# Integer feed-forward of a fused layer stack: gate products first, up products inside the sigmoid pass

## What is computed

```python
def act_qdq(x):
    qmax = 2.0 ** (ACT_BITS - 1) - 1.0
    scale = jnp.maximum(jnp.max(jnp.abs(x)) / qmax, 1e-12)
    return jnp.clip(jnp.round(x / scale), -qmax - 1.0, qmax) * scale
...
x = act_qdq(x)
up = act_qdq(x @ lpbq_dequant(w_up).T)
gate = act_qdq(x @ lpbq_dequant(w_gate).T)
sig = fixed_qdq_u16(jax.nn.sigmoid(gate))
gate = act_qdq(gate * sig)
o = act_qdq(gate * up)
return o @ lpbq_dequant(w_down).T
```

## Time and profile before

| | us |
|---|---|
| median of 3 runs | 2077.92 |
| lowest and highest | 2074.67, 2086.87 |
| span of the profiled execution, first to last instruction | 2076.4 |
| stretch with the gate and up block | 1437 to 1532 |
| stretch with the first gating pass | 1532 to 1573 |
| stretch with the second gating pass | 1573 to 1608 |

### The profile page before, as it was taken

One profiled execution on the slowest core, in us unless ns is written; L12 is line 12 of the kernel. 1 busy time (PEld: TensorE's weight loads), 2 busy tenths in 40 slices (PEclk: granted clock), 3 DMA queues, 4 the chain that ended last, 5 costly groups with the idle time before them and its releaser, 6 DMA issues. The chain is left out here.

```text
span 2076.4 us, 39090 instructions
## 1 busy us (share of the span) xinstructions
PE 1875.1 (90%) x13707; PEld 1519.3 (73%) x13708; DVE 1271.4 (61%) x4668; ACT 835.2 (40%) x2278; POOL 274.0 (13%) x498
## 2 busy tenths in 40 slices
PE   8899998999998989999999988997952989999978
PEld 6567666776767979999999977875531877777745
DVE  7878867778873541111111145676769529999988
ACT  3433336556652111111111102773477524444468
POOL 2001112000001160000000063331000230000022
PEclk9999999999997999999999998998975989999989
DMA  6211111211104421231222021111000031111100
GB/s 224 87 59 47 46 51 67 82 41 42 59 24 155 154 98 59 86 103 66 86 83 86 23 68 42 45 45 62 0 0 0 1 93 44 36 37 39 23 11 31
DMA packets 106722, 124.95 MB, mean 60 GB/s; under 512 B 36160, under 2 KB 85832, under 8 KB 104776
## 3 DMA queue, kind: packets, MB, share of 16 engines
q1 hardware_dynamic: 95704, 107.64, 15.6%
q0 software_dynamic: 3072, 8.39, 1.3%
q10 hardware_dynamic: 7792, 6.95, 1.0%
HBM read 86.39 MB, written 36.63 MB: 59 GB/s over the span
## 5 line engine op out<-in xcount | busy, mean ns | idle before, releaser
L1788 DVE TENSOR_TENSOR me_h<-me_sg,me_ps_u 128x512 f32<-128x512 f32 x106 | 72.5, 686 | 287.3 <-PE me_ps_u L1611 272.0
L1744 ACT ACTIVATE me_sg<-me_ps_g 128x512 f32<-128x512 f32 x106 | 63.3, 597 | 370.4 <-PE me_ps_g L1611 340.3
L1276 ACT ACTIVATE ca_e<-ca_scored,ca_neg_max 128x256 f32<-128x256 f32 x256 | 127.2, 499 | 109.1 <-DVE ca_neg_max L1335 109.1
L1611 PE MATMUL me_ps_g<-me_x_turned,me_w 128*128 128x128 f32 x1184 | 144.8, 276 | 1.9 <-issue 1.9
L1611 PE MATMUL me_ps_u<-me_x_turned,me_w 128*128 128x128 f32 x1184 | 145.4, 276 | 0.0
L1611 PEld LDWEIGHTS me_ps_g<-me_x_turned,me_w 128*128 128x128 f32 x1184 | 141.2, 192 | 4.2 <-issue 2.1
L1618 PE MATMUL me_ps_y<-me_w,me_h 128*128 128x256 f32 x592 | 140.0, 379 | 0.0
L1611 PEld LDWEIGHTS me_ps_u<-me_x_turned,me_w 128*128 128x128 f32 x1184 | 139.4, 193 | 0.0
L2979 ACT ACTIVATE sc_y_all<-ss_v 128x16 f32<-128x16 f32 x256 | 60.8, 238 | 156.1 <-DVE ss_v L3042 156.1
L1618 PEld LDWEIGHTS me_ps_y<-me_w,me_h 128*128 128x128 f32 x592 | 106.8, 190 | 11.4
L1335 DVE CUSTOM_DVE_ANT_0 ca_scored<-ca_main,ca_mask_add 128x256 f32<-128x256 f32 x256 | 92.9, 418 | 20.9 <-PE ca_main L1219 20.9
(11 more groups left out here) (444 smaller groups left out, 4371.6 us busy)
## 6 DMA issues: line engine op xcount, KB each, us to landing
me_w<-in_L_ffn_w_e SPq DMA_DIRECT2D x24, 1024.0 KB, 7.5
ca_k_list<-kv_out SPq DMA_DIRECT2D x28, 256.0 KB, 2.3
ca_v_list<-kv_out SPq DMA_DIRECT2D x28, 256.0 KB, 2.3
sk_gb<-scan_g_band SPq DMA_DIRECT2D x14, 512.0 KB, 3.7
moe_x_list<-me_zeros SPq DMA_DIRECT2D x1, 5248.0 KB, 21.1
me_x_tile<-moe_x_list SPq DMA_DIRECT2D x38, 128.0 KB, 2.0
moe_y_list<-me_y ACTq DMA_DIRECT2D x37, 128.0 KB, 1.7
ca_kT<-ca_k_list SPq DMA_DIRECT2D x4, 1024.0 KB, 4.9
```

Of the source, the lines that this page charges most:

```text
L1276: nc.scalar.activation(e[:, g % 3, e_, it, :], scored[:, g % 2, e_, it, :], ACT.Exp, scale=-1.0, bias=neg_max[:, g % 2, n:n + 1], accum_ou ...
L1611: last = nc.tensor.matmul(ps[:, j * P:(j + 1) * P], w[:, n, kt, f:f + P], x[:, kt, :], start=(kt == 0), stop=(kt == KD - 1))
L1744: nc.scalar.activation(sg[:, c, :], ps_g[c][:, :], ACT.Silu).then_inc(done, 1)
L1788: nc.vector.tensor_tensor(h[:, c, :, :].rearrange("p j n -> p (j n)"), sg[:, c, :], ps_u[c][:, :], ALU.mult).then_inc(done[c], 1)
```

## The change

The two blocks `int_gate_up` and `int_gating` become one, `int_gate_first`, with tile prefix `ig`, no barrier inside it.

- First loop: TensorE makes the gate products alone, one accumulator of 768 columns (two banks) per tile, two such accumulators in turn, filled by pieces of 512 and 256 columns. VectorE takes one maximum over 768 columns per tile and ScalarE makes one copy. x transposed is kept for all tiles, in the place of x normalised.
- The sums and the clipping of the next layer's weights come in this loop. The weights lie in the upper half of `up`, which is not yet used then.
- The scale of gate alone is made. Then the second loop: the sigmoid pass as before, and beside it the up products: TensorE multiplies, VectorE takes the maximum, ScalarE copies. All 16 groups of the next layer's weights are turned in this loop, one per tile.
- The scales of gate * sig and of up are made together, in four VectorE steps on two columns.
- Third loop: the pass with up, as before, but with all up integers made in it. The filler matmuls wait for the product of tile 12 of this loop.

```diff
-        int_gate_up(nc, core, ins, wT, scal, magic, gate, up, tern)
-        int_gating(nc, core, scal, magic, gate, up, tern)
+        int_gate_first(nc, core, ins, wT, scal, magic, gate, up, tern)
         int_down(nc, core, tg, wdT, scal, magic, gate)
...
+def int_gate_first(nc, core, ins, wT, scal, magic, gate, up, tern):
...
+    RING = 4
+    WARM = 28
+    WARM_AT = TILES - 4
+    CUTS = ((0, 512), (512, FF))
...
+        nat = up[:, TILES // 2:TILES, :].rearrange("p t f -> p (t f)").rearrange("p (w n) -> p w n", w=3)
+        xT = core.xn
...
+        ps = [st.ps(f"ps{j}", [P, 1024]) for j in range(2)]
+        next_ps = [st.ps(f"next{j}", [P, 512]) for j in range(2)]
+        idle = st.ps("idle", [P, 512])
...
+            def turn_x(t):
+                pe.wait_ge(x_ready, t + 1)
+                if t >= 1:
+                    pe.wait_ge(xT_ready, t)
+                for kt in range(KD):
+                    last = nc.tensor.transpose(ps_x[:, kt * P:(kt + 1) * P], xi[:, t % 2, kt * P:(kt + 1) * P],
+                                               core.ident[:, :])
+                last.then_inc(x_ps, 1)
+            def multiply(w, t, done):
+                for lo, hi in CUTS:
+                    for kt in range(KD):
+                        last = nc.tensor.matmul(ps[t % 2][:, lo:hi], xT[:, t, kt * P:(kt + 1) * P], wT[:, w, kt, lo:hi],
+                                                start=(kt == 0), stop=(kt == KD - 1))
+                last.then_inc(done, 1)
+            def gate_product(t):
+                pe.wait_ge(xT_ready, t + 1)
+                if t >= 2:
+                    pe.wait_ge(gate_kept, t - 1)
+                multiply(0, t, gate_mm)
+            def up_product(t):
+                if t < 2:
+                    pe.wait_ge(gate_kept, TILES + t - 1)
+                else:
+                    pe.wait_ge(up_kept, t - 1)
+                multiply(1, t, up_mm)
+            def turn_next(g):
+                blocks = parts[g][0]
+                if g >= 2:
+                    pe.wait_ge(copied, g - 1)
+                for j, src in enumerate(blocks):
+                    last = nc.tensor.matmul(next_ps[g % 2][:, j * P:(j + 1) * P], src, ident16[:, :],
+                                            start=True, stop=True)
+                last.then_inc(filled, 1)
+            pe.wait_ge(x_max, 1)
+            nc.tensor.transpose(ps_x[0:1, 0:P], xmax[:, :], core.ident[:, :]).then_inc(x_row, 1)
+            pe.wait_ge(x_one, 1)
+            nc.tensor.matmul(ps[0][:, 0:1], one[:, :], xone[:, :], start=True, stop=True).then_inc(x_all, 1)
+            pe.wait_ge(xsteps, 2)
+            turn_x(0)
+            for t in range(TILES):
+                if t + 1 < TILES:
+                    turn_x(t + 1)
+                gate_product(t)
+            pe.wait_ge(ident_ready, 1)
+            for t in range(TILES):
+                up_product(t)
+                turn_next(t)
+            pe.wait_ge(product, TILES + WARM_AT)
+            for _ in range(WARM):
+                nc.tensor.matmul(idle[:, 0:P], core.ident[:, :], core.ident[:, :], start=True, stop=True)
...
+            def copy_x(t):
+                act.wait_ge(x_ps, t + 1)
+                nc.scalar.activation(xT[:, t, :], ps_x[:, 0:D], ACT.Copy).then_inc(xT_ready, 1)
+            def keep_gate(t):
+                act.wait_ge(gate_maxed, t + 1)
+                nc.scalar.activation(gate[:, t, :], ps[t % 2][:, 0:FF], ACT.Copy).then_inc(gate_kept, 1)
+            def keep_up(t):
+                act.wait_ge(up_maxed, t + 1)
+                nc.scalar.activation(up[:, t, :], ps[t % 2][:, 0:FF], ACT.Copy).then_inc(up_kept, 1)
...
+            def copy_next(g):
+                out = parts[g][1]
+                act.wait_ge(filled, g + 1)
+                nc.scalar.activation(out, next_ps[g % 2][:, 0:out.shape[1]], ACT.Copy).then_inc(copied, 1)
...
+            for u in range(TILES + 1):
+                if u < TILES:
+                    copy_x(u)
+                if u >= 2:
+                    keep_gate(u - 2)
+                if u in (9, 11, 13):
+                    ternary((u - 9) // 2)
+            nc.scalar.preload_act_table(ACT.Sigmoid)
+            keep_gate(TILES - 1)
+            act.wait_ge(gate_scaled, 1)
+            integers(0)
+            for t in range(TILES):
+                if t + 1 < TILES:
+                    integers(t + 1)
+                sigmoid(t)
+                keep_up(t)
+                if t >= 1:
+                    copy_next(t - 1)
+            copy_next(TILES - 1)
+            act.wait_ge(all_scaled, 1)
+            for t in range(TILES):
+                gate_integers(t)
+                up_integers(t)
...
+            def gate_max(t):
+                dve.wait_ge(gate_mm, t + 1)
+                nc.vector.tensor_reduce(gate_top[:, t:t + 1], ps[t % 2][:, 0:FF], AX.X, ALU.max,
+                                        apply_absolute_value=True).then_inc(gate_maxed, 1)
...
+            quant(0)
+            quant(1)
+            for t in range(TILES):
+                if t + 2 < TILES:
+                    quant(t + 2)
+                gate_max(t)
+                if t in (1, 2, 3):
+                    bit_sum(t - 1)
+                if t == 5:
+                    bit_scale()
+                if 6 <= t <= 11:
+                    bit_clip((t - 6) // 2, (t - 6) % 2)
+            link = ends.turn(dve, 0).link
+            dve.wait_ge(gate_maxed, TILES)
+            link(nc.vector.tensor_reduce(most[:, 0:1], gate_top[:, :], AX.X, ALU.max))
+            dve.wait_ge(reached, 1)
+            link(nc.vector.tensor_scalar(scal[:, 4:5], reach[:, 0:1], scal[:, 0:1], 1.0 / QMAX, ALU.mult, ALU.mult))
+            link(nc.vector.tensor_scalar(scal[:, 2:3], scal[:, 4:5], 1e-12, None, ALU.max))
+            link(nc.vector.reciprocal(scal[:, 5:6], scal[:, 2:3]))
+            nc.vector.tensor_scalar(scal[:, 6:7], scal[:, 5:6], scal[:, 0:1], None, ALU.mult).then_inc(gate_scaled, 1)
...
+            up_max(0)
+            up_max(1)
+            sigmoid_integers(0)
+            for t in range(TILES):
+                if t >= 1:
+                    product_max(t - 1)
+                if t + 1 < TILES:
+                    sigmoid_integers(t + 1)
+                if t + 2 < TILES:
+                    up_max(t + 2)
+                dve.wait_ge(si_ready, t + 1)
+                nc.vector.tensor_tensor(gate[:, t, :], gi[:, t % RING, :], si[:, t % 2, :], ALU.mult
+                                        ).then_inc(product, 1)
+            dve.wait_ge(up_maxed, TILES)
+            link(nc.vector.tensor_reduce(most[:, 2:3], up_top[:, :], AX.X, ALU.max))
+            product_max(TILES - 1)
+            dve.wait_ge(product_maxed, TILES)
+            link(nc.vector.tensor_reduce(most[:, 1:2], act_top[:, :], AX.X, ALU.max))
+            dve.wait_ge(reached, 2)
+            link(nc.vector.tensor_tensor(inverse[:, :], reach[:, 1:3], unit[:, :], ALU.mult))
+            link(nc.vector.tensor_scalar(scale[:, :], inverse[:, :], 1.0 / QMAX, 1e-12, ALU.mult, ALU.max))
+            link(nc.vector.reciprocal(inverse[:, :], scale[:, :]))
+            nc.vector.tensor_tensor(to_int[:, :], inverse[:, :], unit[:, :], ALU.mult).then_inc(all_scaled, 1)
...
+            for t in range(TILES):
+                if t >= 1:
+                    product_max(TILES + t - 1)
+                dve.wait_ge(gi_ready, TILES + t + 1)
+                dve.wait_ge(ui_ready, t + 1)
+                nc.vector.tensor_tensor(gate[:, t, :], gi[:, t % RING, :], ui[:, t % RING, :], ALU.mult
+                                        ).then_inc(product, 1)
+            product_max(2 * TILES - 1)
+            dve.wait_ge(product_maxed, 2 * TILES)
+            link(nc.vector.tensor_reduce(most[:, 3:4], out_top[:, :], AX.X, ALU.max))
+            dve.wait_ge(reached, 3)
...
+            for step, (lo, hi) in ((1, (0, 1)), (8, (1, 3)), (13, (3, 4))):
+                pool.wait_ge(ends.sem, step)
+                nc.gpsimd.partition_all_reduce(reach[:, lo:hi], most[:, lo:hi], P, bass.bass_isa.ReduceOp.max
+                                               ).then_inc(reached, 1)
```

More of the change, by code:

```diff
@@ L2369, in int_gate_up @@
                                                                          "xT_ready"))
[L2370 to L2371 removed]
+        w_in = [st.sem(f"w_in{w}") for w in range(3)]
+        summed, reduced, clipped, bits = st.sem("summed"), st.sem("reduced"), st.sem("clipped"), Chain(st.sem("bits"), 8)
+        gate_mm, gate_maxed, gate_kept = (st.sem(n) for n in ("gate_mm", "gate_maxed", "gate_kept"))
@@ L2432, in ternary, with integers @@
                 nc.scalar.activation(tern[:, w, :], nat[:, w, :], ACT.Identity, bias=minus_magic[:, :])
-            for u in range(1, TILES + 2):
-                if u <= TILES:
-                    copy_x(u - 1, (u - 1) % 2)
-                if u >= 2:
-                    keep(u - 2, u % 2)
-                if u in (10, 12, 14):
```

(19 more changed lines are left out.)

263 lines of the change are left out of this document (66 added, 197 removed).

## The result

| | before, us | changed, us |
|---|---|---|
| median (4 runs each) | 2078.14 | 2058.85 |
| lowest and highest | 2074.67, 2086.87 | 2056.22, 2061.76 |
| span of the profiled execution | 2076.4 | 2060.0 |

The ratio is 0.990 (0.9878 to 0.9923): faster, by 19.3 us, with an interval of 16.0 to 25.4. Run twice more on other occasions beside the kernel before, the unchanged program gave ratios of 0.9882 (0.9862 to 0.9902) and 0.9884 (0.9855 to 0.9912), 23.4 and 22.6 us between the medians. The forecast was 2053.7, which is 24.2 us less than the median of 2077.9 that it started from, with a range of 2047 to 2066.

The account below looks back on a forecast made before the run. TensorE was taken to bound the gate and up block, VectorE the gating passes. Gains of 37.7 and 0.8 us less losses of 13.6 and 0.7 made 24.2 off 2077.9: 2053.7, range 2047 to 2066.

Parts of the forecast that it names:

- First loop: Gate products alone on TensorE: 2.82 us a tile, 49.1 us from first matmul to last gate maximum, against 86.8 before.
- The stalls: In the first loop, three weight-sum tiles hold up TensorE, 3.0 us, plus 0.3 for the clipping tiles.
- The first tile: Start of the first loop: it runs slower than later tiles, by 0.94 us as before the change.
- The prices of the 768-wide instructions: One 768-column maximum on VectorE takes 0.96 us, one such copy (keep) on ScalarE 0.82, extended from 384-column times.
- Scales, second and third loop: Gate scales 2.7 us; sigmoid loop with up products, through its scales, 56.3; up pass to its last product 29.7.
- The step-by-step start of the second loop: Sigmoid loop with up products: first gated product starts 6.9 us after the first gate integers, against 4.75 before.
- Differences carry over one to one: Whole span: time saved in the changed part shows fully in the total, since everything behind it starts after a barrier.
- Down block: Its low-clock start: filler matmuls about 1.5 us nearer give back between 0 and 3.3 us; 0 was taken.
- Rival A: Second loop: hand-overs between engines wait, 4.4 us a tile instead of 3.19, 16 us of gain lost, 2069.5; chance 0.10.
- Rival B: Second loop: TensorE's clock stays at 1.2 GHz, 5.73 us a tile, 41.5 us lost, 2095.2, slower than before; chance 0.04.
- The argument against B from the busy share: Second loop: TensorE would be busy about 88% of 3.19 us, and at 84% busy its clock was 1.00.
- Rival C: First loop paced by VectorE's quantise, maximum, keep chain: tiles near 4.3 us instead of 2.82, 2076; chance 0.04.

## Why the prediction was right, and where its sizes were off

- What bounds each stretch: right. TensorE paced the first loop (but for the sum and clipping tiles), VectorE the second, as the kernel without the up maximum showed by speeding up (136.6) and the one with doubled up products by slowing down (179.8).
- First loop, 49.1 forecast, 51.3 measured: the one term of the block that was mis-sized. A plain tile was 2.80 for 2.82. The stalls came to 4.6 us for 3.3: the first sum tile 1.3, the other two 0.9 and 1.0, and three clipping tiles 0.45 each (3.25 for 2.80) where I had put 0.3 in all. I had set the clipping tiles at "about 2.8", level with TensorE's 2.82, and hid them; every second one stalls TensorE for 0.45 us. The first tile lost 2.11 us (4.86 - 2.75) instead of 0.94, as the clock was at 0.50 in the 8 us up to 1449. Two lines of TensorE's timeline and four of VectorE's show a clipping tile that stalls:

```profile
1469.46 0.38 PE L2408 MATMUL ig_ps_x<-ident,ig_xi 128*128 128x128 f32 x2
...
1472.66 0.44 PE L2408 MATMUL ig_ps_x<-ident,ig_xi 128*128 128x128 f32 x2 [0.23 <-DVE ig_xi L2550]
```

```profile
1469.66 0.96 DVE L2555 TENSOR_REDUCE ig_gate_top<-ig_ps 128x1 f32<-128x768 f32 x1 [0.62 <-PE ig_ps L2415]
1470.54 1.28 DVE L2591 TENSOR_SCALAR if_up<-if_up,ig_inv 128x2048 f32<-128x2048 f32 x1
1471.85 0.35 DVE L2545 TENSOR_SCALAR ig_xr<-x_norm,if_scal 128x256 f32<-128x256 f32 x1
1472.31 0.29 DVE L2550 TENSOR_SCALAR ig_xi<-ig_xr 128x256 f32<-128x256 f32 x1
```

  VectorE's list in it comes to about 2.85 us, but it cannot begin before the product is done: it waits 0.62 us, starts 0.20 behind TensorE's transposes, and has x ready 2.94 later, at 1472.60. So the next transposes come 3.20 us after the last ones and not 2.80, and the products 3.25 (1469.68 to 1472.93). In the tile behind it the maximum does not wait (1472.52), and x is ready at 1475.26, before TensorE wants it. The step that was mis-sized took the sum of a list for the length of a chain that starts with a wait.
- The prices of the 768-wide instructions fitted, but not by the working beside them. 554 ns and half of 0.95 us make 1.03, not 0.96, and 491 ns and half of 0.92 make 0.95, not 0.82; the runs have 0.95 to 0.96 and 0.81. With 1.03 VectorE's period would have been 3.26 us and the second loop about 1 us longer. To that extent the second loop's forecast was better than its working.
- Scales, second and third loop: 2.6, 56.2 and 29.7 for 2.7, 56.3 and 29.7. The step-by-step start of the second loop was right to 0.2 us: the first product began 7.1 after the first integers.
- "Differences carry over one to one": not met in the first pair of profiles, where the block gained 22.5 us and the span 16.4, since parts that nobody changed moved by 6.1, 4.4 of it in the tail. The tail goes with TensorE's clock at the scan's opening, which is at the 1.2 GHz level there for a longer or shorter time in each execution; the part ahead of the block and the down block with what follows it drift as well. The medians do not show a lasting loss: 19.3 us (16.0 to 25.4), then 23.4 (20.4 to 28.7) and 22.6 (18.3 to 30.2), and 24.2 lies in each interval. So the step is neither refuted nor shown to the last 5 us.
- Down block: 0 forecast. Its start to the scan's opening took 96.7 us in the first profile, 98.9 and 98.6 in the repeats, and 97.6, 96.6 and 97.1 in the three profiles with the old block; a cost or a gain of 1 us would not be seen.
- Rival A (loads that do not mesh): refuted by VectorE's closed chain, by ScalarE's idle time of 0.24 to 0.45 us a tile and by the kernel without the up maximum. Rival B (clock): the clock stood at 0.94 over the loop with the idle end of it included, and at 1.00 up to there:

```profile
1499.00:1548.00 49.00, 44.04 (x164) 23.43 (x162) 45.53 (x58) 44.09 (x63) 0.00 (x0) 1.00 0.00 1
```

  The argument against B from the busy share was weak, though: beside the line with 84% at 1.00, has one with 6.54 of 8.00 us (82%) at 0.50. B did not come, but those rows could not have ruled it out. The Trainium skill, "TensorE: Matmul & The Clock Gate", section "A second HAM failure mode: psum-queue depth-cycling", was the page that spoke for it. No oscillation was seen here, with two PSUM accumulators in turn and idle moments of 0.3 us, in any of the profiles. B's price of 41 us was near: the doubled kernel's block lost 35.4 at 5.44 a tile, where B had 5.73. Rival C is refuted by the plain tile's 2.80.

## What to carry to other kernels

Where one stage idles one engine and the next stage idles another, move the work that nothing downstream needs yet, and forecast the merged loop from start-to-start distances of each engine's own list, engine by engine: here that gave its length to 0.1 us in 56. In a loop that gets shorter, side work that was free under the long tile (a 2.3 us sum) is the first thing to stall it. Cutting it up took 1.9 us off the block at the same clock, too little to show in the time, and 1.0 us was lost again where the moved pieces ended up. An engine's list gives the length of a tile only if its first instruction does not wait; else count from the end of that wait. Before blaming a change for a loss in an untouched stage, compare that stage in several executions of both kernels.

## What the runs showed of the hardware

- The part ahead of the block, the same in all kernels, took 1441.5 to 1450.2 us in twelve profiles, and the part from the scan's opening 368.3 to 374.5: an end-to-end difference of 5 us needs the stretches as well.
- At the scan's opening TensorE waits 3.9 to 4.8 us for its first z and can then run at 1.2 GHz for long although it stands still no more. In the first profile of the changed kernel it is busy 20.2 of the 24.0 us from 1688, with PEclk 0.50, and the rest is the wait up to 1691.81; in the sigmoid loop, with an idle moment in every tile, it had 1.00 (44.0 of 49 us busy). First the row of TensorE, then the window:

```profile
1691.81 1.06 PE L3129 MATMUL ss_ps_z<-ident,ss_z 128*32 128x128 f32 x4 [4.83 <-DVE ss_z L3064]
```

```profile
1688.00:1712.00 24.00, 20.19 (x82) 17.02 (x83) 17.54 (x128) 7.12 (x37) 0.00 (x0) 0.50 0.10 28
```

  With twenty small matmuls in that wait, PEclk over the first 40 us was 0.94 to 1.00 in three kernels, against 0.67 to 0.87 in the nine profiles without.
- Matmul pieces of 512 and 256 columns ran at the same rate per column as pieces of 384: a tile of 3072 columns took 2.80 us with its transposes, one of 6144 columns 5.38, which leaves 2.58 for 3072 columns and 0.22 for the transposes.
